# One block for the three programs of each engine, in a kernel of cached cross-attention, self-attention and a mixture of experts

## The chip, the cores and the metric

The kernel runs on one core of one Trainium2 chip. A core has five engines that each run a program of their own: TensorE (PE in the rows, with its weight loads as PEld), VectorE (DVE), ScalarE (ACT), GpSimd (POOL) and SyncE (SP), which here only issues DMAs. They order their work among themselves by semaphores. The metric is the device time of one execution in microseconds (us), taken as the median of several; lower is better.

## The reference, cut to what matters

```python
# 1. cross-attention of 512 rows of x to a context of 8192 rows, width 1024
Q, K_new, V_new = x @ Wq.T + bq, x @ Wk.T + bk, x @ Wv.T + bv      # x is layer-normed first
K = concat(ctx[:7680], K_new); V = concat(ctx[:7680], V_new)       # the last 512 rows are replaced
h = x + softmax(Q @ K.T / sqrt(1024) + mask) @ V
# 2. causal self-attention, 16 query and 4 key heads of 64, low-rank additions, rotary positions
h = h + self_attention(layernorm(h))
# 3. shared feed-forward (relu squared, 2048 wide) + 2 of 16 experts (512 wide) a token
out = h + shared(layernorm(h)) + routed_experts(layernorm(h))
```

All is float32. A product is made of three passes of a rounded kind: each operand is split in a high part, made by ACT with a copy, and a low part, made by DVE as the difference (`_hi`, `_lo`), and the product is high·high + high·low + low·high (L32, L33 and L34 of the helper `matmul_3pass`).

## The kernel before, in words

The kernel is written by hand, engine by engine. Three functions are called in a row: `cross_projections` (V, Q and K of the 512 rows; tiles are named a_...), `attention` (64 steps over 16 context blocks of 512 rows and 4 query blocks of 128 rows, then the self-attention; names b_... and c_...), and `ffn` (names d_... and e_...). Each opens a `with nc.Block() as block:` (L157, L585, L1682) and gives in it one program to each engine (`@block.sync`, `@block.gpsimd`, `@block.tensor`, `@block.scalar`, `@block.vector`). The order of the work in such a program is written out; no scheduler changes it. At the end of a block every engine drains and meets the others at a barrier, and only then does each branch into its program of the next block. I call these two places the first border (around 155 us) and the second border (around 1127 us).

What stands around the first border. The projections run in 12 half-groups; the last two make the K of the 512 rows, feature tiles 4 to 7. For each output tile PE signals `out_ready`, DVE adds the bias (L376) into `a_tmp`, ACT makes the high part (L311), DVE the low part (L379), and the latter counts in the semaphore `out_lo`: 8 V pieces, 8 Q tiles and 8 K tiles make 24. `a_tmp` and the bias rows `a_bv_rows` lie in the same memory as the mask tiles `b_scores`. POOL ends its program by storing four blocks of low-rank-corrected weights (L211). In `attention`, POOL first loads four mask tiles (L626), clears a tile (L627) and goes on with tables; PE begins step 0 of the scores, which goes over the 8 feature tiles f of K and Q (`scores`, L737 onward); SP waits for `kv_split` before it loads more of the cache (L590).

What stands around the second border. PE turns the last 128 rows of the normed hidden state (`turn_xn`, L996); ACT (L1169) and DVE (L1406) split them, and `xt_lo_done` reaches 8. In `ffn`, PE makes the router's logits for these rows (`route_rows`, L423 and L424, 16 products of 128 columns), then the first half of `unit(0)`, which is 12 products, then it turns the logits (`turn_logits`, L1823), and for that it waits until ACT has copied them from PSUM (L2040). ACT's program of `ffn` begins with `shared_hi(2)` (L1986), the high part of the third piece of the shared weights, and the copy of the logits stands behind it. SP's program of `ffn` begins with the load of that piece, `load_shared(2)` (L1688), which waits for the low part of piece 0 (`s_split`, made by DVE at L1411 in `attention`), then piece 3, then the store of the normed rows (L1715). The last DMAs of SP in `attention` are the loads of pieces 0 and 1 (L621).

The lines that the steps touch:

```python
                pe.wait_ge(s["xt_lo_done"], 2 * TB)
                route_rows(pe, bank[:, LOGIT_BANK, :], F, 3 * P, T).then_inc(s["logits_ready"], 1)
...
                shared_hi(2)
                act.wait_ge(s["logits_ready"], 1)
                act.activation(lT, bank[:, LOGIT_BANK, :], ACT.Copy).then_inc(s["lg_read"], 1)
                shared_hi(3)
```

Of the kernel before, what the change touches and what calls it, by code (L numbers as in the profile page):

```python
# [14 lines left out]
P = 128  # L15
# [86 lines left out]
def cross_projections(nc, m, ins, resid, QT, K, V, raw, at, kv_loaded, ident, ln, weff, weff_stored):  # L102
# [23 lines left out]
    with ExitStack() as stage:  # L126
# [30 lines left out]
        with nc.Block() as block:  # L157
            @block.sync
            def _(sp):
                def load_x(t):  # L160
                    sp.dma_start(resid[:, t, :], ins["x"][t]).then_inc(x_loaded[t], 16)

                def load_half(h):
                    sp.dma_start(raw[:, 0, h * D:(h + 1) * D],
                                 ins["xattn_w"][0][:, h * D:(h + 1) * D]).then_inc(w_first if h == 0 else w_loaded[0], 16)

                load_x(0)
                load_x(1)
                load_half(0)
                load_x(2)  # L170
                load_half(1)
                load_x(3)
                for w in range(1, HALVES):
                    if w >= 2:
                        sp.wait_ge(w_split, w + 2)
                    sp.dma_start(raw[:, w % 2, :], ins["xattn_w"][w]).then_inc(w_loaded[w % 2], 16)
                for n in range(2):
                    sp.wait_ge(w_split, HALVES + 2 + n)
                    sp.dma_start(raw[:, n, :], ins["kv"][n]).then_inc(kv_loaded[n], 16)

            @block.gpsimd
            def _(pool):
                pool.memset(consts[:, 0:1], LN_EPS).then_inc(consts_done, 1)
                pool.memset(consts[:, 1:2], -0.5).then_inc(consts_done, 1)
                make_identity(pool, ident, ident_done)
                pool.wait_ge(consts_done, 2)

                def first_weights_lo(j):
                    pool.wait_ge(w_hi_done, j + 1)
                    pool.tensor_tensor(w_buf(K_lo, 0)[:, j, :], w_feature(raw, 0, j), f32(w_buf(K_hi, 0)[:, j, :]),  # L190
                                       ALU.subtract).then_inc(w_split, 1)

                ln.rstd(pool, 0, mean_var, rstd, consts, 0)
                ln.rstd(pool, 0, mean_var, rstd, consts, 1)
                first_weights_lo(0)
                first_weights_lo(1)
                ln.rstd(pool, 0, mean_var, rstd, consts, 2)
                first_weights_lo(2)
                first_weights_lo(3)
                ln.rstd(pool, 0, mean_var, rstd, consts, 3)  # L200
                pool.dma_start(b_cols[:, :], ins["xattn_b_cols"]).then_inc(bias_loaded, 16)
                pool.dma_start(bv_rows[:, :], ins["xattn_bv"].to_broadcast([P, D])).then_inc(bias_loaded, 16)
                pool.dma_start(stack_mask[:, :], ins["stack_mask"][:, 2:4]).then_inc(bias_loaded, 16)
                pool.dma_start(p_raw[0:3 * RANK, :, :], ins["attn_p"]).then_inc(bias_loaded, 16)
                for n in range(4):
                    if n:
                        pool.wait_ge(weff_stored, 16 * n)
                    pool.dma_start(w_block[:, :, :], ins["attn_w"][6 + n].rearrange("p (b n) -> p b n", n=W)
                                   ).then_inc(block_loaded, 16)
                    pool.wait_ge(low_done, LOW_SPLIT + 4 * n + 4)  # L210
                    pool.dma_start(weff[n].rearrange("p (b n) -> p b n", n=W), w_block[:, :, :]).then_inc(weff_stored, 16)  # L211

            @block.tensor
            def _(pe):
                pe.wait_ge(ident_done, 2)

                def turn_x(t):
                    pe.wait_ge(ln.xn_done, t + 1)
                    for h in range(2):
                        n = 2 * t + h  # L220
                        if n >= 2:
                            pe.wait_ge(xt_lo_done, n - 1)
                        for i in range(4):
                            e = 4 * h + i
                            mm = pe.transpose(bank[:, 6 + n % 2, i * P:(i + 1) * P],
                                              resid[:, t, e * P:(e + 1) * P], ident[:, :])
                        mm.then_inc(xt_ready, 1)

                def low_products(n):

                    if n == 0:
                        pe.wait_ge(low_done, LOW_SPLIT)
                    pe.wait_ge(biased, 4 * n + 4)
                    for i in range(4):
                        e = 4 * (n % 2) + i
                        pe.matmul(bank[:, 4 * (n % 2) + i, :], p_s[0:3 * RANK, 0, e * P:(e + 1) * P],
                                  p_s[0:3 * RANK, 1, (n // 2) * W:(n // 2 + 1) * W],
                                  start=True, stop=True).then_inc(low_ready, 1)

                turn_x(0)  # L240
                turn_x(1)
                for w in range(HALVES):
                    g, h = divmod(w, 2)
                    if h == 1 and 1 <= g <= 4:
                        low_products(g - 1)
                    if w:
                        pe.wait_ge(w_split, w + 4)
                    for i in range(4):
                        o = 4 * g + i
                        if h == 0 and g >= 2:  # L250
                            pe.wait_ge(biased, o - 7)
                            pe.wait_ge(low_done, LOW_SPLIT + o - 7)
                        if g == 1 and h == 0 and i >= 2:
                            pe.wait_ge(xt_lo_done, 2 * TB)
                        if g == 0:
                            pe.wait_ge(xt_lo_done, 2 * i + h + 1)
                        for j in range(4):
                            e = 4 * h + j
                            if w == 0:
                                pe.wait_ge(w_split, j + 1)  # L260
                            if g >= 2:
                                lhs = [w_buf(x, w)[:, j, i * P:(i + 1) * P] for x in (K_hi, K_lo)]
                                rhs = [xT_hi[:, e, :], xT_lo[:, e, :]]
                            else:
                                lhs = [x[:, e, i * P:(i + 1) * P] for x in (xT_hi, xT_lo)]
                                rhs = [w_buf(x, w)[:, j, :] for x in (K_hi, K_lo)]
                            mm = matmul_3pass(bank[:, 4 * (g % 2) + i, :], *lhs, *rhs,
                                              first=e == 0, last=e == DB - 1)(pe)
                        if h == 1:
                            mm.then_inc(out_ready, 1)  # L270
                        if w == 0 and i < 2:
                            turn_x(i + 2)
                    if h == 0:
                        mm.then_inc(w_used, 1)

            @block.scalar
            def _(act):
                def weights_hi(w):
                    act.wait_ge(w_loaded[w % 2], 16 * (w // 2 + 1))
                    if w >= 2:  # L280
                        if w % 2 == 0:
                            act.wait_ge(w_used, w // 2)
                        else:
                            act.wait_ge(out_ready, 4 * (w // 2))
                    act.activation(w_buf(K_hi, w), raw[:, w % 2, :].rearrange("p (e n) -> p e n", n=W),
                                   ACT.Copy).then_inc(w_hi_done, 1)

                def first_weights_hi(j):
                    act.wait_ge(w_first if j < 2 else w_loaded[0], 16)
                    act.activation(w_buf(K_hi, 0)[:, j, :], w_feature(raw, 0, j), ACT.Copy).then_inc(w_hi_done, 1)  # L290

                first_weights_hi(0)
                first_weights_hi(1)
                for n in range(2 * TB):
                    t, h = divmod(n, 2)
                    if n == 2:
                        first_weights_hi(2)
                    if n == 3:
                        first_weights_hi(3)
# [2245 lines left out]
```

## Time and profile before

| | us |
|---|---|
| median of 3 runs | 1452.84 |
| the three runs | 1451.96, 1455.63, 1452.84 |
| the profiled execution | 1451.73 |
| its span, from the first to the last instruction | 1450.1 |
| PE busy in it | 1408.3 (97%) |
| DVE, ACT, POOL busy | 845.6, 530.3, 202.8 |

The profiled execution took 1.63 us more than its span, and 1.11 us less than the median of the three runs. PE is busy in nearly all of the span; each instruction of it starts before the one ahead has ended by the profile's model, so a steady run of products of 512 columns shows a start every 0.23 us, while one is listed with 0.39 us. Time on PE's path is therefore counted from start to start.

### The profile page before, as it was taken

The page shows a single profiled execution, that of the slowest core. Times are in us where ns is not written, and L with a number is a line of the kernel's source. Part 1 is how long each engine was busy: PE and PEld are TensorE (multiplying, and loading weights), DVE is VectorE, ACT ScalarE, POOL GpSimd, SP SyncE. Part 2 cuts the span into 40 slices and gives each one's busy share as a digit, 9 for nine tenths or more (in the row PEclk, how much of TensorE's full clock was granted, in tenths as well). Part 3 has the DMA queues.
Part 4 walks back from the last instruction along what each step waited for, and adds up shares of the span by engine and source line. Part 5 has one row for each costly group of instructions (what it writes and reads, how often), then busy time and mean ns, then how long its engine had stood idle before and what let it go on. Part 6 is the DMA issues. An engine that isn't in the chain of part 4 may idle for free. (4 is left out here: it accounts for less than half of the span.)

```text
span 1450.1 us, 18196 instructions
## 1 busy us (share of the span) xinstructions
PE 1408.3 (97%) x6676; PEld 1151.2 (79%) x6676; DVE 845.6 (58%) x1232; ACT 530.3 (37%) x947; POOL 202.8 (14%) x264
## 2 busy tenths in 40 slices
PE   7999999999999999999999999899999899998998
PEld 5878788888888888888888888776778788887786
DVE  5554455555555455455554557678765676676655
ACT  3222322332223322223222223556432435665561
POOL 3000100000000000000000000455311022122132
PEclk9999999999999999999999999999999999999999
DMA  7453643333333333333333322201100566886766
GB/s 251 152 202 118 247 176 118 116 109 108 123 123 111 113 108 115 131 108 116 108 112 131 108 98 77 107 1 59 34 1 1 175 210 228 299 294 222 266 224 218
DMA packets 43487, 203.64 MB, mean 140 GB/s; under 512 B 5233, under 2 KB 5297, under 8 KB 31985
## 3 DMA queue, kind: packets, MB, share of 16 engines
q1 hardware_dynamic: 30016, 152.32, 30.1%
q0 software_dynamic: 9568, 36.35, 7.7%
q10 hardware_dynamic: 3840, 14.16, 2.5%
q8 instruction: 37, 0.61, 0.2%
q14 instruction: 26, 0.20, 0.0%
HBM read 182.36 MB, written 20.45 MB: 140 GB/s over the span
## 5 line engine op out<-in xcount | busy, mean ns | idle before, releaser
L32 PE MATMUL banks<-V_hi,b_PT_hi 128*128 128x512 f32 x512 | 205.6, 401 | 0.0
L1024 ACT ACTIVATE b_PT_hi<-banks 128x512 fp32r<-128x512 f32 x64 | 38.3, 599 | 446.9 <-PE banks L757 446.9
L32 PE MATMUL banks<-K_hi,QT_hi 128*128 128x512 f32 x512 | 199.3, 389 | 2.5 <-PEq L157 2.5
L34 PE MATMUL banks<-V_hi,b_PT_lo 128*128 128x512 f32 x512 | 200.2, 391 | 0.0
L33 PE MATMUL banks<-V_lo,b_PT_hi 128*128 128x512 f32 x512 | 199.6, 390 | 0.0
L34 PE MATMUL banks<-K_hi,QT_lo 128*128 128x512 f32 x512 | 199.4, 389 | 0.0
L33 PE MATMUL banks<-K_lo,QT_hi 128*128 128x512 f32 x512 | 199.2, 389 | 0.0
L1247 DVE TENSOR_TENSOR b_scores<-banks,b_scores 128x512 f32<-128x512 f32 x64 | 44.2, 691 | 202.0 <-PE banks L34 202.0
L642 POOL DMA_DIRECT2D b_scores<-mask x60 | 32.2, 537 | 639.2 <-PE banks L757 621.4
L2176 DVE TENSOR_TENSOR e_lo<-e_raw,e_hi 128x1024 fp32r<-128x1024 f32 x80 | 95.2, 1231 | 38.4 <-ACT e_hi L2012 37.3
L32 PEld LDWEIGHTS banks<-K_hi,QT_hi 128*128 128x128 f32 x512 | 96.1, 188 | 22.8 <-issue 2.9
L34 PEld LDWEIGHTS banks<-V_hi,b_PT_lo 128*128 128x128 f32 x512 | 96.1, 188 | 21.0
L34 PEld LDWEIGHTS banks<-K_hi,QT_lo 128*128 128x128 f32 x512 | 96.1, 188 | 20.0
L33 PEld LDWEIGHTS banks<-K_lo,QT_hi 128*128 128x128 f32 x512 | 96.1, 188 | 19.9
L33 PEld LDWEIGHTS banks<-V_lo,b_PT_hi 128*128 128x128 f32 x512 | 96.4, 188 | 18.5
L32 PEld LDWEIGHTS banks<-V_hi,b_PT_hi 128*128 128x128 f32 x512 | 96.2, 188 | 18.0
L1267 DVE TENSOR_TENSOR V_lo<-raw,V_hi 128x2048 fp32r<-128x2048 f32 x30 | 68.8, 2292 | 64.4 <-ACT V_hi L1048 64.4
L1267 DVE TENSOR_TENSOR K_lo<-raw,K_hi 128x2048 fp32r<-128x2048 f32 x30 | 68.8, 2293 | 61.8 <-ACT K_hi L1048 61.8
L2012 ACT ACTIVATE e_hi<-e_raw 128x1024 fp32r<-128x1024 f32 x80 | 81.4, 1060 | 23.0 <-DMA e_raw<-w_down 16.1
L1204 DVE SCALAR_TENSOR_TENSOR resid<-resid,b_alpha,banks 128x1024 f32<-128x1024 f32 x60 | 76.5, 1275 | 6.8 <-PE banks L34 6.8
L32 PE MATMUL banks<-K_hi,V_hi 128*128 128x512 f32 x160 | 68.2, 427 | 0.8 <-ACT c_piece L1069 0.8
L34 PE MATMUL banks<-K_hi,V_lo 128*128 128x512 f32 x160 | 64.0, 400 | 0.0
(327 smaller groups left out, 2752.4 us busy)
## 6 DMA issues: line engine op xcount, KB each, us to landing
raw<-kv SPq DMA_DIRECT2D x60, 1024.0 KB, 4.7
e_raw<-w_up SPq DMA_DIRECT2D x40, 512.0 KB, 5.0
e_raw<-w_down SPq DMA_DIRECT2D x40, 512.0 KB, 5.9
b_scores<-mask POOLq DMA_DIRECT2D x64, 256.0 KB, 2.9
d_s_raw<-shared_w SPq DMA_DIRECT2D x32, 512.0 KB, 4.9
raw<-xattn_w SPq DMA_DIRECT2D x11, 1024.0 KB, 4.9
y_dram<-c_zeros ACTq DMA_DIRECT2D x1, 6656.0 KB, 28.0
raw<-attn_w SPq DMA_DIRECT2D x6, 1024.0 KB, 4.7
```

The source lines that it names most:

```text
L32: pe.matmul(out, lhs_hi, rhs_hi, start=first, stop=False)
L33: pe.matmul(out, lhs_hi, rhs_lo, start=False, stop=False)
L34: return pe.matmul(out, lhs_lo, rhs_hi, start=False, stop=last)
L642: pool.dma_start(s_sb[:, u, :], ins["mask"][it * 4 + u]).then_inc(mask_loaded[u], 16)
L1024: act.activation(PT_hi[:, u % 2, :], T_ps[:, u % 2, :], ACT.Copy).then_inc(b["pt_hi"], 1)
L1204: op = dve.scalar_tensor_tensor(resid[:, qb, :], resid[:, qb, :], alpha[:, qb:qb + 1], O_ps(u), ALU.mult, ALU.add)
L1247: dve.tensor_tensor(s_sb[:, u % 4, :], S_ps[:, u % 2, :], s_sb[:, u % 4, :], ALU.add).then_inc(b["masked"], 1)
L1267: dve.tensor_tensor(split_tile(False, u), raw_tile(u), f32(split_tile(True, u)), ALU.subtract).then_inc(b["kv_split"], 1)
L2012: act.activation(e_hi[:, first + j, :], e_raw[:, j, :], ACT.Copy).then_inc(s["e_hi"], 1)
L2176: dve.tensor_tensor(e_lo[:, first + j, :], e_raw[:, j, :], f32(e_hi[:, first + j, :]), ALU.subtract).then_inc(s["e_split"], 1)
```

## The change

The three `with nc.Block()` are replaced by one block that is opened in `build` and handed to the three functions. The second and third programs of an engine follow its first without drain and barrier. Where the first barrier had kept apart reads and writes of the same memory, waits on `out_lo` (handed over as `own_split`) are added: PE waits in step 0 before each feature tile, and POOL before each of the four first mask loads. Nothing is added at the second border. The diff, without the change of indentation (all lines of the functions' bodies keep their order):

```diff
-def cross_projections(nc, m, ins, resid, QT, K, V, raw, at, kv_loaded, ident, ln, weff, weff_stored):
+def cross_projections(nc, block, m, ins, resid, QT, K, V, raw, at, kv_loaded, ident, ln, weff, weff_stored):
...
-        with nc.Block() as block:
             @block.sync
...
+        return out_lo
...
-        with nc.Block() as block:
             @block.sync
...
             @block.gpsimd
             def _(pool):
                 for u in range(4):
+                    pool.wait_ge(own_split, 8 if u < 2 else 21 + u)
                     pool.dma_start(s_sb[:, u, :], ins["mask"][u]).then_inc(mask_loaded[u], 16)
...
                     for f in range(DB):
+                        if known == 0:
+                            pe.wait_ge(own_split, 17 + f)
                         mm = matmul_3pass(S_ps[:, u % 2, :],
...
-        with nc.Block() as block:
             @block.sync
...
+            block = stage.enter_context(nc.Block())
+            own_split = cross_projections(nc, block, m, ins, resid, QT, K, V, raw, at, kv_loaded, ident, ln, weff, weff_stored)
             d, F = ffn_semaphores(m), ffn_tiles(m, at, stage)
             F["bank"] = m.psum("banks", [P, 8, W], stack=stage)
-            attention(nc, m, ...)
-            ffn(nc, m, ...)
+            attention(nc, block, m, ..., own_split)
+            ffn(nc, block, m, ...)
```

On PE at the first border, before: the last products of the projections, the two branches with the barrier between them, and the first products of step 0.

```order
L33 MATMUL a_banks<-V_lo,K_hi 128x512
L34 MATMUL a_banks<-V_hi,K_lo 128x512
L157 UNCONDITIONAL_BRANCH
L737 UNCONDITIONAL_BRANCH [waits barrier_Pool_Activation_PE_DVE_SP_release]
L32 MATMUL banks<-K_hi,QT_hi 128x512
L33 MATMUL banks<-K_lo,QT_hi 128x512
L34 MATMUL banks<-K_hi,QT_lo 128x512
L32 MATMUL banks<-K_hi,QT_hi 128x512
```

And the same place of the changed kernel:

```order
L33 MATMUL a_banks<-V_lo,K_hi 128x512
L34 MATMUL a_banks<-V_hi,K_lo 128x512
L737 UNCONDITIONAL_BRANCH
L32 MATMUL banks<-K_hi,QT_hi 128x512 [waits a_out_lo]
L33 MATMUL banks<-K_lo,QT_hi 128x512
L34 MATMUL banks<-K_hi,QT_lo 128x512
L32 MATMUL banks<-K_hi,QT_hi 128x512 [waits a_out_lo]
```

One branch and the barrier are gone; each feature tile of step 0, one in three products, has a wait of its own.

On SP at the second border, before (d_s_raw holds the pieces of the shared weights as loaded):

```order
L621 DMA d_s_raw<-shared_w 128x1024 [waits c_qk_ready]
L621 DMA d_s_raw<-shared_w 128x1024
L585 UNCONDITIONAL_BRANCH
L1683 UNCONDITIONAL_BRANCH [waits barrier_Pool_Activation_PE_DVE_SP_release]
L1688 DMA d_s_raw<-shared_w 128x1024 [waits d_s_split] x2
L1715 DMA xn_dram<-e_raw 128x4x1024 [waits ln_xn_done]
```

And in the changed kernel, where the lines have other numbers:

```order
L620 DMA d_s_raw<-shared_w 128x1024 [waits c_qk_ready]
L620 DMA d_s_raw<-shared_w 128x1024
L1684 UNCONDITIONAL_BRANCH
L1689 DMA d_s_raw<-shared_w 128x1024 [waits d_s_split] x2
L1716 DMA xn_dram<-e_raw 128x4x1024 [waits ln_xn_done]
```

The loads of pieces 2 and 3 now stand behind `s_split` alone, and no longer behind the barrier too.

## Rows read from the trace of the kernel before

**Rows 1.** Span of the core and mean granted clock of TensorE.
```profile
core 0: 1450.1 us, clock 0.994
```

**Rows 2.** Waits of PE: who waited for whom, total us, times, longest.
```profile
PE banks L32 <- DVE d_s_lo L2155: 5.9, 2, 4.7
PE banks L32 <- PEq L157: 2.5, 1, 2.5
...
PE banks L1823 <- ACT e_xg L2040: 1.2, 1, 1.2
```

**Rows 3.** PE in order of time: start, us, operation [idle before <- releaser].
```profile
134.07 0.39 PE L34 MATMUL a_banks<-V_hi,K_lo 128*128 128x512 f32 x1
134.30 0.39 PE L32 MATMUL a_banks<-V_hi,K_hi 128*128 128x512 f32 x1
...
153.11 0.39 PE L34 MATMUL a_banks<-V_hi,K_lo 128*128 128x512 f32 x1
156.00 0.47 PE L32 MATMUL banks<-K_hi,QT_hi 128*128 128x512 f32 x1 [2.50 <-PEq L157]
```

**Rows 4.** Line 157, the first border: ns min/median/max, first and last start.
```profile
L157 PEldq DRAIN  x1: 4267/4267/4267, 149.3 to 149.3; - x1
L157 PEldq EVENT_SEMAPHORE  x1: 51/51/51, 155.9 to 155.9; - x1
```

**Rows 5.** DVE before the first border: low parts of K tiles 6 and 7.
```profile
152.27 0.69 DVE L379 TENSOR_TENSOR K_lo<-a_tmp,K_hi 128x512 fp32r<-128x512 f32 x1 [0.70 <-ACT K_hi L311]
...
154.98 0.69 DVE L379 TENSOR_TENSOR K_lo<-a_tmp,K_hi 128x512 fp32r<-128x512 f32 x1 [0.70 <-ACT K_hi L311]
```

**Rows 6.** POOL at the first border.
```profile
156.40 2.13 POOL L626 DMA_DIRECT2D b_scores<-mask  x4 [33.07 <-POOLq L157]
```

**Rows 7.** PE at the second border, in order of time.
```profile
1125.40 1.09 PE L996 MATMUL banks<-ident,e_raw 128*128 128x128 f32 x8 [0.69 <-DVE e_raw L96]
1128.34 0.30 PE L423 MATMUL banks<-d_xT_hi,e_hi 128*128 128x128 f32 x1 [1.85 <-PEq L585]
...
1130.15 0.45 PE L32 MATMUL banks<-d_xT_hi,d_s_hi 128*128 128x512 f32 x1
...
1132.71 0.39 PE L34 MATMUL banks<-d_xT_hi,d_s_lo 128*128 128x512 f32 x1
1134.29 0.66 PE L1823 MATMUL banks<-ident,e_xg 128*128 128x128 f32 x4 [1.19 <-ACT e_xg L2040]
```

**Rows 8.** DVE at the second border.
```profile
1118.13 2.35 DVE L1411 TENSOR_TENSOR d_s_lo<-d_s_raw,d_s_hi 128x1024 fp32r<-128x1024 f32 x2
...
1126.72 1.29 DVE L1406 TENSOR_TENSOR d_xT_lo<-banks,d_xT_hi 128x512 fp32r<-128x512 f32 x2 [1.38 <-ACT d_xT_hi L1169]
```

**Rows 9.** ACT at the second border.
```profile
1126.09 1.08 ACT L1169 ACTIVATE d_xT_hi<-banks 128x512 fp32r<-128x512 f32 x2 [7.06 <-PE banks L996]
1132.70 1.06 ACT L1986 ACTIVATE d_s_hi<-d_s_raw 128x1024 fp32r<-128x1024 f32 x1 [5.52 <-DMA d_s_raw<-shared_w]
1133.66 0.58 ACT L2040 ACTIVATE e_xg<-banks 128x512 f32<-128x512 f32 x1
```

**Rows 10.** The chain that ended last, in order of time: start, us, what.
```profile
1128.30 4.38 DMA d_s_raw<-shared_w
...
1276.34 0.47 PE banks L32
...
1304.06 0.24 PE banks L34
...
1322.10 0.80 PE banks L32
```

**Rows 11.** Windows: us, busy us of PE, PEld, DVE, ACT, POOL, granted clock, DMA.
```profile
943.00:946.00 3.00, 3.00 (x8) 2.06 (x7) 1.72 (x4) 2.71 (x20) 1.99 (x2) 0.50 0.00 0
...
1322.00:1325.00 3.00, 2.90 (x7) 2.21 (x8) 1.78 (x3) 2.53 (x4) 0.00 (x0) 0.50 0.42 165
153.00:156.00 3.00, 0.50 (x3) 0.10 (x2) 1.44 (x2) 0.63 (x1) 0.00 (x0) 1.00 0.00 0
```

More of the change, by code:

```diff
@@ new lines, in after, with project @@
+            def after(n):
+                transpose(0, n - 1, n - 1)
+                values(0, n - 2, n - 2)
+                turn_x(0)
+                values(0, n - 1, n - 1)
+                turn_x(1)
+            passes(pe, step, after)
+            def project(g, t, first, last, out):
+                rows = slice(t * P, (t + 1) * P)
+                for e in range(first, last):
+                    pe.wait_ge(s["w_split"], 2 * g + e // 4 + 1)
+                    mm = matmul_3pass(out, xT_hi[:, e, rows], xT_lo[:, e, rows],
+                                      K_hi[:, g % 2, e, :], K_lo[:, g % 2, e, :],
+                                      e == 0, g >= 3 and e == DB - 1)(pe)
+                return mm
@@ new lines, in low_rank, with project_low @@
+            def low_rank():
+                pe.wait_ge(s["table_split"], 1)
+                pe.wait_ge(s["xt_lo"], 2 * TB)
+                pe.wait_ge(b["acc_done"], STEPS)
+                for e in range(DB):
+                    mm = matmul_3pass(bank[:, 6, :], A_hi[:, e, :], A_lo[:, e, :], xT_hi[:, e, :], xT_lo[:, e, :],
+                                      e == 0, e == DB - 1)(pe)
+                mm.then_inc(s["lr_ready"], 1)
+            def project_low(i):
+                g, t = ORDER[i]
+                out, rows = piece_bank(i), slice(t * P, (t + 1) * P)
+                if i == 0:
+                    pe.wait_ge(s["lr_lo"], 2)
+                    pe.wait_ge(s["table_split"], 3)
+                mm = pe.matmul(out, lr_s[:, rows], B_s[:, g, :], start=False, stop=g == 0)
+                if g:
+                    mm = pe.matmul(out, lr_lo[:, rows], B_m[:, g, :], start=False, stop=True)
+                mm.then_inc(s["out_ready"], 1)
@@ new lines, in heads_transpose @@
+            def heads_transpose(u):
+                pe.wait_ge(s["s_exp"], u + 1)
+                if u >= 1:
+                    pe.wait_ge(s["pt_act"], u)
+                    pe.wait_ge(s["pt_dve"], u)
+                else:
+                    pe.wait_ge(s["qk_read"], 5)
+                for h in range(2):
+                    for k in range(keys_of(u) // P):
+                        mm = pe.transpose(bank[:, h, k * P:(k + 1) * P],
+                                          p_sb[:, u % 2, h, k * P:(k + 1) * P], ident[:, :])
+                mm.then_inc(s["pt_ready"], 1)
@@ new lines, in heads_values @@
+            def heads_values(u):
+                g = 2 * (u % PAIRS) // GROUP
+                pe.wait_ge(s["pt_act"], u + 1)
+                pe.wait_ge(s["pt_dve"], u + 1)
+                if u == 0:
+                    pe.wait_ge(s["piece_copied"], AHEAD)
+                k = 2 * (u + 2)
+                if not slot_read(pe, k) and not slot_read(pe, k - 1) and u >= 1:
+                    pe.wait_ge(s["y_done"], u)
+                keys = keys_of(u) // P
+                for h in range(2):
+                    for k in range(keys):
+                        mm = pe.matmul(bank[:, Y_BANK, h * HD:(h + 1) * HD],
+                                       pT_sb[:, u % 2, h, k * P:(k + 1) * P], v_sb[:, k, g * HD:(g + 1) * HD],
+                                       start=k == 0, stop=k == keys - 1)
+                mm.then_inc(s["y_ready"], 1)
@@ new lines, in turn_y, with slot @@
+            def turn_y(n):
+                t, h = divmod(n - 2 * TB, 2)
+                pe.wait_ge(s["y_out"], HKV * (t + 1))
+                for i in range(4):
+                    e = 4 * h + i
+                    mm = pe.transpose(xt_bank(n)[:, i * P:(i + 1) * P], y[:, t, e * P:(e + 1) * P], ident[:, :])
+                mm.then_inc(s["xt_ready"], 1)
+            def slot(k):
+                if k not in PIECE_SLOTS.values() and k not in ROWS_SLOTS.values():
+                    return
+                step = k // 2
+                if k % 2 or not slot_read(pe, k - 1):
+                    if step - 1 - (k % 2 == 0) >= 1:
+                        pe.wait_ge(s["y_done"], step - 1 - (k % 2 == 0))
+                for i, at_slot in PIECE_SLOTS.items():
+                    if at_slot == k:
+                        turn_piece(i)
+                for n, at_slot in ROWS_SLOTS.items():
+                    if at_slot == k:
+                        turn_y(n)
@@ new lines, in fill @@
+            def fill(st, part):
+                n, third = divmod(st if st < 3 * FILLED else st - 1, 3)
+                if st == 3 * FILLED:
+                    return
+                blocks_of = FILL_PARTS[third][part]
+                for e in blocks_of:
+                    if n >= FILLED:
+                        output(n - FILLED, e, e + 1)
+                        continue
+                    i = AHEAD + n
+                    g, t = ORDER[i]
+                    if e == 0:
+                        pe.wait_ge(s["piece_copied"], i if n else TB)
+                    mm = project(g, t, e, e + 1, bank[:, FILL_BANK, :])
+                    if e == DB - 1:
+                        if t == TB - 1:
+                            mm.then_inc(s["group_done"], 1)
+                        project_low(i)
@@ new lines, in output @@
+            def output(o, first, last):
+                t, c = divmod(o, 2)
+                for e in range(first, last):
+                    if e % 4 == 0:
+                        pe.wait_ge(s["xt_lo"], 2 * TB + 2 * t + e // 4 + 1)
+                    if e == 0:
+                        pe.wait_ge(s["add_done"], min(o, 2 * TB - 2)) if o else pe.wait_ge(s["piece_copied"], PIECES)
+                    mm = project(3 + c, t, e, e + 1, out_bank(o))
+                if last == DB:
+                    mm.then_inc(s["out_ready"], 1)
```

3374 lines of the change are left out of this document (1633 added, 1741 removed).

## The prediction, made before the changed kernel had run

> **What bounds the kernel now.** I read the granted clock and span first, then PE's waits, then the two borders on every engine in order of time, then the chain that ended last. The span is 1450.1 us at a mean granted clock of 0.994 [rows 1], and PE is busy in 97% of it, so the end is set by PE's own stream and only what moves that stream counts. PE's waits are few. Two of them are the borders, 2.5 us released by the semaphore of line 157 and 1.85 us by that of line 585, and 1.2 us stand at the turning of the logits, behind ACT [rows 2, 7]. The larger wait for the shared weights, 5.9 us in two pieces, lies much later. In the 64 steps of cached attention between the borders the waits of PE name nothing, so what PE gains at the first border has nothing in the loop that would take it back.
>
> **First border: removed.** The last product of the projections starts at 153.11, the first of the scores at 156.00 [rows 3]. In a steady run starts are 0.23 apart (134.07 and 134.30 in the same group), so without the border the next start would be 153.34: 156.00 - 153.34 = 2.66 us on PE's path. What held PE was DVE, whose low part of the last K tile ran 154.98 to 155.67 [rows 5], then its drain and the barrier, released at 155.9 [rows 4].
>
> **First border: added waits.** PE now waits in step 0 before each feature tile. Tile f needs f + 17 counts. Each tile is three products, 0.68 us, so tile 6 is reached at 153.34 + 6 x 0.68 = 157.4, and it needs DVE's tile 6, which ended at 152.27 + 0.69 = 152.96; tile 7 is reached at 158.1 and needs the one that ended at 155.67 [rows 5]. The margin is 2.4 us, so none of the eight is late. What a wait that is already met costs: the product at 134.30 has two such waits, on the bias and on the low-rank sums, and starts 0.23 after the one ahead, like its neighbours [rows 3]. I take zero; behind a waiting tile only PE's own following products are queued. The bounds are 0 and, were the last tile late after all, the 2.66 gained here, since DVE's time sets when PE can go on.
>
> POOL's four mask loads get waits too. Before, they were issued from 156.40 on, 2.13 us for the four [rows 6]. Mask 0 and 1 need 8 counts, reached long before; mask 2 needs 23 (152.96) and mask 3 needs 24 (155.67). So all four go out earlier than before. Behind the fourth are POOL's clearing of a tile and with it ACT's filling of `y_dram`, and the tables; SP waits for a semaphore of the attention steps either way. The clearing follows mask 3, so it comes 156.40 + 2.13 - (155.67 + 0.53) = 2.3 us earlier, where PE comes 2.66 earlier: no engine falls behind by more than 0.4 us, and PE reads nothing of it for a long time. Cost nothing; cover if this fails: the two whole score steps before PE needs the first result of DVE and ACT.
>
> **First border: the branch.** One branch stays on each engine. PE's first product of the scores starts at 156.00, the barrier's event is listed at 155.9 with 51 ns [rows 4], so a branch into the next program has cost PE at most 0.1 us there. PE's sequencer also ran ahead: its drain started at 149.3, while PE's last product started at 153.11 [rows 3, 4]. So some 3.8 us of a late branch would be hidden now. I take zero, with 0 and 0.1 as bounds from these rows. The Trainium skill, "Runtime: NRT & Kernel Launch", section "Instruction fetch mechanics", speaks against the change here: it says that a taken branch whose target is outside the pages held makes the sequencer fetch code before it goes on. By that rule the barrier might have been the cover of such a fetch. The rows show the branch behind the barrier, and no such stall after it.
>
> **Second border: removed.** PE turns eight blocks from 1125.40 and begins the logits at 1128.34 [rows 7]. But their first product also waits for the low parts of these rows, and DVE makes them from 1126.72 to 1128.01 [rows 8]. From ACT's end at 1133.66 + 0.58 to PE's start at 1134.29 there are 0.05 us [rows 7, 9]; with that or a little more the start becomes 1128.1 and the gain is 0.24 us, not the 1.85 that the row of the wait shows. Bounds: 0 (another 0.3 us of signal) and 0.33 (no delay).
>
> **Second border: the logits.** This is the step that isn't seen in the row of the border. PE's twelfth product of unit 0 starts at 1132.71, so the turning of the logits could start at 1132.94; it starts at 1134.29 [rows 7]: 1.35 us lost. PE waits for ACT's copy of the logits at 1133.66, and this stands behind ACT's high part of piece 2 at 1132.70, which waited for its load [rows 9]. SP issued that load at 1128.30, right after the barrier, and it took 4.38 us [rows 10]. In the changed kernel the load waits only until DVE is done with piece 0, the first of two that ran from 1118.13 for 2.35 us [rows 8], so it is issued at about 1119.4 and lands at about 1123.8 (all in the old times). ACT ends its last split of rows at 1126.09 + 1.08 = 1127.17 [rows 9], makes the high part of piece 2 until 1128.2, and copies the logits as soon as PE has made them. These are 16 products from 1128.1 on. Unit 0 starts at 1132.71 + 0.23 - 12 x 0.23 = 1130.2 before, so at about 1129.9 now; the copy takes 0.58 and is done by 1130.7, two microseconds before PE asks for it at 1132.7. The gain is the whole 1.35. Bounds: 0, if the copy is late all the same, and 1.35.
>
> More is earlier behind it: the low parts of pieces 2 and 3, the routing on DVE and the loads that follow come some 3 to 5 us earlier against PE's 4. The first of PE's two waits on line 2155 ends at 1276.34, far behind [rows 10], so that brings nothing, and the store of the normed rows beside them delays nothing of PE either.
>
> **Is it given back?** The largest wait of PE behind this, 4.7 us up to 1322.10, is fed by a load; the chain goes from PE's product at 1304.06 through ACT, DVE, SP and a DMA back to PE [rows 10]. Such a chain begins at PE, so it moves with PE and the gain stays. I give nothing back.
>
> **Sum.** 2.66 + 0.24 + 1.35 = 4.25 us. The profiled execution took 1451.73 (its span and 1.63 around it), so it would take 1447.5; the median of the runs shown, 1452.84, lies 1.11 above it and would become 1448.6. I predict 1448.0, halfway, since I cannot say which of the two executions the next ones resemble.
>
> **The rivals.**
> - The clock gives more. In 943 to 946 and in 1322 to 1325 PE ran at a granted clock of 0.50, the lower of the two levels (1.2 GHz), the second right after the wait of 4.7 us; between 153 and 156, with PE busy 0.50 of 3 us, the clock stayed at 1.00 [rows 11]. The mean of 0.994 makes (1 - 0.994) x 2 x 1450 = 17 us at the lower clock, 9 us lost. The runs shown differ by 3.7 us, and I take that for such stretches. In an execution where the pause of a border did lower the clock, the change removes that too: 3.4 us at half speed, 1.7 us lost, is my estimate from these windows, each of which is half speed over its whole 3 us. Then 1447.5 - 1.7 = 1445.8, and down to 1445.0 with two. The Trainium skill, "TensorE: Matmul & The Clock Gate", part 1, says that the chip's looking is not aligned with the kernel, so one and the same pause may or may not lower the clock; this case's one trace can neither show nor refute it.
> - Only part of it. If ACT still reaches the logits late (a load delayed, the copy behind something else), only 2.66 + 0.24 is gained: 1448.8 to 1449.9. The row of ACT's load wait, 5.52 us long [rows 9], speaks for the full gain; the margin of two microseconds would have to go.
> - The change doesn't do what it says: PE stops at tile 7, because DVE's last low part comes later than before, or the gain is swallowed at 1322. Then 1451.7 to 1452.8. DVE has nothing new to do at the border and the chain starts at PE, both against it.
> - Slower: the clock goes the other way. All of PE's later pauses shift by 2.7 to 4.3 us against whatever lowers the clock, and where a pause now keeps the clock up it may lower it. The place is the self-attention from 880 to 1110 and the expert chunks, where PE pauses often. It costs 1.7 us a stretch, and decides against the change from the third additional one on: 1448.0 + 3 x 1.7 = 1453.1. Nothing in the rows says that a shift favours more stretches over fewer.
>
> **How the numbers follow.** Full gain with the clock as before: 0.62, own range 1446.6 to 1449.6. More from the clock: 0.16. Part of it: 0.14. No gain: 0.04. Slower through the clock: 0.04. A measurement of this kernel can tell about 0.3% from no change, 4.4 us, which puts the line at 1448.5, right beside my forecast. Of the full gain I put two thirds below it, 0.41; with the 0.16 that makes 0.57 for faster. The rest of the full gain, the partial and the missing gain, and most of the slower case, which only passes +0.3% (1457.2) with five or more stretches, make 0.41 for the same; 0.02 for slower. The range for 8 in 10: 1445.3 to 1450.6, which leaves out the missing gain, the slower case and the end of the clock's.
>
> **What would show it.** On PE, products 0.23 us apart from the projections into the scores, no wait on line 157's semaphore, and no wait on `out_lo`; SP's load of piece 2 about 9 us before the turning of the last rows is done; PE's wait at the logits gone, and a start of them about 0.1 us after DVE's last low part; the wait before the shared weights in the fifth chunk still there, some 4.3 us earlier in the span. I am wrong if PE stops in step 0, if ACT's copy of the logits is still what PE waits for, or if PE's waits later than 1250 grow by what was gained.

## The result, and the profile after

| | before | changed |
|---|---|---|
| median of 9 executions, us | 1452.20 | 1447.86 |
| lowest and highest | 1450.29, 1455.63 | 1446.55, 1452.75 |
| profiled execution | 1451.73 | 1449.44 |
| its span and mean granted clock | 1450.1, 0.994 | 1447.5, 0.991 |

The ratio is 0.997, with a 95% interval from 0.9958 to 0.9983: 4.3 us faster, where 4.25 were summed and 1448.0 was predicted. The whole interval lies below 1, so the gain is real, though it is right at the 0.3% that I had set as the bound.

The span of the profiled execution fell by only 2.6 us, and its clock is lower. So the size can't be read off the two spans; it has to be taken apart by steps. The lines of the changed kernel have other numbers than before (L422 and L423 are the logits, L1824 their turning, L626 the mask loads, L378 the low part of the K tiles).

The first border, PE in order of time, answers to [rows 3]:

```profile
152.77 0.39 PE L33 MATMUL a_banks<-V_lo,K_hi 128*128 128x512 f32 x1
153.00 0.39 PE L34 MATMUL a_banks<-V_hi,K_lo 128*128 128x512 f32 x1
153.23 0.39 PE L32 MATMUL banks<-K_hi,QT_hi 128*128 128x512 f32 x1
153.45 0.39 PE L33 MATMUL banks<-K_lo,QT_hi 128*128 128x512 f32 x1
...
157.99 0.39 PE L32 MATMUL banks<-K_hi,QT_hi 128*128 128x512 f32 x1
158.21 0.39 PE L33 MATMUL banks<-K_lo,QT_hi 128*128 128x512 f32 x1
```

The scores follow 0.23 us behind the projections, and feature tile 7, reached at 157.99, starts without a pause. DVE's low part of that tile, which answers to [rows 5], and POOL's last two mask loads, which answer to [rows 6], in order of time:

```profile
154.88 0.69 DVE L378 TENSOR_TENSOR K_lo<-a_tmp,K_hi 128x512 fp32r<-128x512 f32 x1 [0.70 <-ACT K_hi L310]
```

```profile
153.15 0.54 POOL L626 DMA_DIRECT2D b_scores<-mask  x1 [28.86 <-DVE K_lo L378]
155.87 0.54 POOL L626 DMA_DIRECT2D b_scores<-mask  x1 [2.18 <-DVE K_lo L378]
156.40 0.97 POOL L627 MEMSET c_zeros<- 128x1024 f32 x1
```

DVE is done at 155.57, 2.4 us before PE needs the tile.

The second border, PE in order of time, answers to [rows 7]:

```profile
1120.84 1.09 PE L998 MATMUL banks<-ident,e_raw 128*128 128x128 f32 x8 [0.70 <-DVE e_raw L96]
1123.51 0.33 PE L422 MATMUL banks<-d_xT_hi,e_hi 128*128 128x128 f32 x1 [1.57 <-DVE d_xT_lo L1408]
...
1126.15 0.63 PE L34 MATMUL banks<-d_xT_hi,d_s_lo 128*128 128x512 f32 x1
1126.58 0.63 PE L32 MATMUL banks<-d_xT_hi,d_s_hi 128*128 128x512 f32 x1
...
1129.74 0.60 PE L1824 MATMUL banks<-ident,e_xg 128*128 128x128 f32 x4
```

From the turned rows to the first logit there are 2.67 us, before 2.94: 0.27 gained, and the pause of 1.57 us that is left is DVE's, no longer the barrier's. The wait at the turning of the logits is gone. But the products ahead of it are 0.43 us apart instead of 0.23, so from the first logit to the turning there are 6.23 us, where before there were 5.95 with the wait in them. ACT, which answers to [rows 9], and SP at the same place:

```profile
1121.53 1.09 ACT L1171 ACTIVATE d_xT_hi<-banks 128x512 fp32r<-128x512 f32 x2 [7.06 <-PE banks L998]
1122.51 1.06 ACT L1987 ACTIVATE d_s_hi<-d_s_raw 128x1024 fp32r<-128x1024 f32 x1
1125.55 0.60 ACT L2041 ACTIVATE e_xg<-banks 128x512 f32<-128x512 f32 x1 [1.98 <-PE banks L423]
```

```profile
1114.81 1.46 SPq L1689 DMA_DIRECT2D d_s_raw<-shared_w  x2
```

ACT no longer waits for the load of piece 2, since SP issues it at 1114.81, and its copy of the logits waits for PE alone. Windows of the changed kernel, which answer to [rows 11] (us, busy us of PE, PEld, DVE, ACT and POOL, granted clock, DMA share, GB/s):

```profile
153.00:156.00 3.00, 3.00 (x15) 2.49 (x14) 1.44 (x2) 0.63 (x1) 0.67 (x2) 1.00 0.27 87
1126.00:1128.00 2.00, 2.00 (x6) 1.51 (x6) 0.88 (x1) 1.09 (x2) 0.00 (x0) 0.50 0.97 299
1153.00:1156.00 3.00, 3.00 (x9) 2.35 (x8) 2.40 (x10) 1.06 (x1) 0.00 (x0) 0.50 0.13 46
1317.00:1323.00 6.00, 5.09 (x12) 3.89 (x13) 4.76 (x5) 5.53 (x6) 0.00 (x0) 0.50 0.32 99
```

The lower of the two levels (1.2 GHz) stands in the stretch right behind the pause of the second border, in another some 27 us later, and for 6 us at 1317 instead of 3 at 1322. Neither of the first two was in the profile before. In the other direction, a stretch of 3.4 us at 991 that the profile before had is missing here. Against the profile before that makes some 6 us more at the lower clock, up to 3 us lost, and this is where the execution lost what its span lacks.

PE's waits (who for whom, total, times, longest) answer to [rows 2]:

```profile
PE banks L32 <- DVE d_s_lo L2156: 4.7, 2, 4.4
...
PE banks L422 <- DVE d_xT_lo L1408: 1.6, 1, 1.6
```

Neither border's semaphore is named any more. The wait for the shared weights is still there.

### The profile page after: what moved, and what is told of

It reads as the page before. It is cut to its first block and busy times, and to the rows that moved or that the text cites. A ratio compares the mean times of both kernels' runs of the same rounds, so it can differ in the third digit from the quotient of the medians.

```text
span 1447.5 us, 18174 instructions
## 1 busy us (share of the span) xinstructions
PE 1411.2 (97%) x6676; PEld 1154.1 (80%) x6676; DVE 846.9 (59%) x1232; ACT 530.2 (37%) x947; POOL 203.1 (14%) x264
```

## The experiments

### The first border alone, and the second alone

```diff
+            with nc.Block() as block:
                 own_split = cross_projections(nc, block, ...)
...
                 attention(nc, block, ..., own_split)
+            with nc.Block() as block:
                 ffn(nc, block, ...)
```

> Projections and attention in one block, the feed-forward in a block of its own: only the first border is gone. My theory: the products of the scores follow 0.23 us after the last of the projections (saving 2.66 us), the second border stays with PE's start 0.3 us behind DVE's last low part, and PE waits 1.2 us at the turning of the logits as before; median 2.7 us under the kernel before. Rival (the borders cost only together, or the barrier moves its wait elsewhere): less than 1 us.

Measured: 1449.45 us (8 executions), ratio to the kernel before on the same chip 0.9977, interval 0.9960 to 0.9995, so 3.3 us faster, with 2.7 inside the interval. The first border behaved as expected (152.82, then 153.04). PE at the second:

```profile
1119.09 1.09 PE L998 MATMUL banks<-ident,e_raw 128*128 128x128 f32 x8 [0.70 <-DVE e_raw L96]
1122.04 0.30 PE L422 MATMUL banks<-d_xT_hi,e_hi 128*128 128x128 f32 x1 [1.85 <-PEq L2472]
1128.24 0.60 PE L1824 MATMUL banks<-ident,e_xg 128*128 128x128 f32 x4
```

The barrier's pause of 1.85 us is there as before. One thing I had expected is not: PE doesn't wait at the turning of the logits, although this border is kept and ACT's copy is as late as ever (it starts 5.4 us behind the first logit, before 5.3). There are 6.20 us between the two lower rows, as many as in the changed kernel within 0.03.

```diff
             with nc.Block() as block:
                 cross_projections(nc, block, ...)
...
             with nc.Block() as block:
                 attention(nc, block, ...)
                 ffn(nc, block, ...)
```

(without the added waits)

> The projections in a block of their own, attention and feed-forward in one: only the second border is gone, and none of the added waits is there. My theory: PE waits 2.5 us at the first border as before; at the second PE starts the logits 0.1 us after DVE's last low part instead of 0.33 us, and the wait of 1.2 us at their turning is gone, 1.6 us in all. Rival (the second border is worth the 1.85 us that its row shows, and the logits' wait is ACT's own): the start comes 1.85 us earlier against the end of the turned rows, and 1.2 us of wait stay.

Measured: 1453.93 us (10 executions), ratio 1.0005, interval 0.9991 to 1.0018. The 1.6 us are not seen; the interval ends at 1.3 us of gain. PE in this kernel:

```profile
1125.85 0.33 PE L422 MATMUL banks<-d_xT_hi,e_hi 128*128 128x128 f32 x1 [1.57 <-DVE d_xT_lo L1405]
...
1128.53 0.63 PE L33 MATMUL banks<-d_xT_lo,d_s_hi 128*128 128x512 f32 x1
1128.95 0.63 PE L34 MATMUL banks<-d_xT_hi,d_s_lo 128*128 128x512 f32 x1
...
1132.10 0.60 PE L1821 MATMUL banks<-ident,e_xg 128*128 128x128 f32 x4
```

All steps of the border are as predicted (a pause of 1.57 us, no wait at the turning), but again the products are 0.42 us apart, and 6.25 us lie between logit and turning. So in these two profiled executions the stretch costs the same, with the border or without it. The two rivals in the expectations don't explain that; the clock does, below.

### The load's place, and ACT's order, with both borders kept

```diff
                 for i in range(2):
                     sp.dma_start(F["s_raw"][:, i, :], ins["shared_w"][i]).then_inc(d[f"s_loaded{i}"], 16)
+                for i in range(2):
+                    sp.wait_ge(d["s_split"], i + 1)
+                    sp.dma_start(F["s_raw"][:, i, :], ins["shared_w"][2 + i]).then_inc(d[f"s_loaded{i}"], 16)
...
-                load_shared(2)
-                load_shared(3)
```

> The kernel before with both borders kept, but SP issues the loads of pieces 2 and 3 of the shared weights at the end of its attention program, behind the low parts of pieces 0 and 1. My theory: the start of the logits stays 0.3 us behind DVE's last low part (border kept), PE's wait of 1.2 us at their turning is gone: 1.35 us gained from the load's place alone. Rival (the barrier itself makes ACT late): the wait stays at about 1.2 us.

```diff
-                shared_hi(2)
                 act.wait_ge(s["logits_ready"], 1)
                 act.activation(lT, bank[:, LOGIT_BANK, :], ACT.Copy).then_inc(s["lg_read"], 1)
+                shared_hi(2)
```

> The kernel before with both borders, but ACT copies the logits before it makes the high part of piece 2. My theory: the copy was late only because it stood behind an instruction that waited for a load, so PE's wait of 1.2 us at the turning is gone though the load is as late as before (issued at the barrier, 4.4 us). Rival (the load itself, or the copy, is what takes the time): the wait stays.

One execution of each, 1456.04 and 1451.74 us. In neither does PE wait at the turning (1128.48 to 1134.70 and 1126.56 to 1132.75, 6.22 and 6.19 us). That is what both expectations say of the wait, but it proves little, since the first-border kernel has no wait there either while its copy is late. These two settle that each edit makes the copy early. The 1.35 us that were expected of the load's place are not shown: one time of each kernel, and in the first a mean clock of 0.989, the lowest of all profiled executions. ACT in the kernel with the early load, where the copy waits for PE alone:

```profile
1128.46 1.06 ACT L1987 ACTIVATE d_s_hi<-d_s_raw 128x1024 fp32r<-128x1024 f32 x1 [1.15 <-PEq L585]
1131.18 0.60 ACT L2041 ACTIVATE e_xg<-banks 128x512 f32<-128x512 f32 x1 [1.66 <-PE banks L424]
```

They show something at the first border, which they keep. The kernel with the copy first, in two windows:

```profile
152.00:155.00 3.00, 1.58 (x7) 0.96 (x6) 1.44 (x2) 0.91 (x2) 0.00 (x0) 1.00 0.00 0
156.00:159.00 3.00, 2.91 (x7) 2.37 (x8) 0.00 (x0) 0.00 (x0) 2.51 (x5) 0.50 0.39 113
```

The pause of the border is followed by the lower clock here. In the profile before it was not, with the same pause [rows 3, 11]:

```profile
156.00:159.00 3.00, 3.00 (x13) 2.52 (x14) 0.00 (x0) 0.00 (x0) 2.60 (x5) 1.00 0.44 153
```

### What the pause at the first border was

```diff
-                        pe.wait_ge(own_split, 17 + f)
+                        pe.wait_ge(own_split, 24)
```

> The changed kernel, but PE waits before the first feature tile of step 0 for all 24 low parts instead of one tile at a time. My theory: the pause at the first border was DVE's tail, 2.3 us, and only 0.3 us the drain and barrier; so PE starts the scores about 0.05 us after DVE's last low part, some 2.4 us later than in the changed kernel, and nearly the whole gain of this border is gone. Rival (the drain and the barrier are the price): PE starts at once or within 1 us.

One execution, 1452.55 us. PE and DVE at the border:

```profile
153.33 0.39 PE L34 MATMUL a_banks<-V_hi,K_lo 128*128 128x512 f32 x1
155.95 0.50 PE L32 MATMUL banks<-K_hi,QT_hi 128*128 128x512 f32 x1 [2.23 <-DVE K_lo L378]
```

```profile
155.21 0.69 DVE L378 TENSOR_TENSOR K_lo<-a_tmp,K_hi 128x512 fp32r<-128x512 f32 x1 [0.70 <-ACT K_hi L310]
```

PE starts at 155.95, 0.05 us behind DVE's end and 155.95 - 153.56 = 2.39 us later than it could. Set against the 2.66 us before, the barrier and its drains were 0.27; 2.39 were the tail of ACT and DVE, and it is the wait tile by tile that gives them back. One block with a single coarse wait would have gained next to nothing at this border. The one time doesn't size this; the rows do.

### The clock behind the second border

```diff
+            shared_split(pe, 0)
+            for e in range(6):
+                pe.matmul(bank[:, 0, :], s_hi[:, 0, e * P:(e + 1) * P], s_hi[:, 0, 0:W], start=True, stop=True)
             pe.wait_ge(s["xt_lo_done"], 2 * TB)
```

> The changed kernel with six products of 512 columns, written to a bank that unit 0 overwrites, in PE's pause before the last logits. They leave the output as it is. They take 6 x 0.23 = 1.4 us of a pause of 1.57 us, so they delay PE by 0 to 0.1 us. Theory: the lowered clock of 3.4 us that follows this pause in the changed kernel's profile comes from the pause; with it filled, no stretch of lowered clock begins between the turned rows and unit 0, and the median is 0 to 1.7 us lower. Rival (it comes from the light stretch around it, or from elsewhere): the lowered stretch is there in this run too, and the median is the same.

Measured: 1444.64 us (12 executions), ratio 0.9953, interval 0.9934 to 0.9973; 3.2 us under the changed kernel, 2.8 under its repetition on another chip. PE:

```profile
1121.56 1.63 PE L1907 MATMUL banks<-d_s_hi 128*128 128x512 f32 x6
1123.38 0.33 PE L422 MATMUL banks<-d_xT_hi,e_hi 128*128 128x128 f32 x1 [0.18 <-DVE d_xT_lo L1408]
...
1127.33 0.39 PE L32 MATMUL banks<-d_xT_hi,d_s_hi 128*128 128x512 f32 x1
1127.56 0.39 PE L33 MATMUL banks<-d_xT_lo,d_s_hi 128*128 128x512 f32 x1
...
1128.02 0.60 PE L1824 MATMUL banks<-ident,e_xg 128*128 128x128 f32 x4
```

The pause is 0.18 us, the clock stays up, and there are 4.64 us from logit to turning. The median moved by more than the 0 to 1.7 us expected: the stretch some 27 us later, at 1153 in the changed kernel, is gone here as well, and two such stretches are 2 x 1.6 = 3.2 us. The size is less sure than the medians look. The twelve times run from 1442.91 to 1455.33, they come from another chip than the repetition of the changed kernel, and the ratio's interval overlaps that of the changed kernel (0.9958 to 0.9983). That the clock is higher with the filler is seen in the means: 0.9943 over these twelve, 0.9924 over the 21 of the changed kernel.

```profile
1126.00:1128.00 2.00, 2.00 (x10) 1.61 (x9) 1.01 (x1) 0.96 (x2) 0.00 (x0) 1.00 0.98 281
1148.00:1152.00 4.00, 4.00 (x31) 3.77 (x31) 1.91 (x8) 2.55 (x4) 0.00 (x0) 1.00 0.64 223
```

To tell the clock from the wait, the same filler went into the kernel with only the first border gone, ahead of the barrier that it keeps.

```diff
                 turn_xn(3)
+                pe.wait_ge(d["s_split"], 1)
+                for e in range(6):
+                    pe.matmul(bank[:, 0, :], F["s_hi"][:, 0, e * P:(e + 1) * P], F["s_hi"][:, 0, 0:W], start=True, stop=True)
```

> Only the first border gone (the feed-forward in a block of its own), with the same six filling products at the end of PE's attention program, ahead of the barrier; they leave the output as it is. It separates the clock from the logits' wait. My theory: with the first border alone gone, PE's wait at the turning of the logits was hidden by the lowered clock, which made PE 1.7 us late itself; with the pause filled the clock stays up, and the wait of 1.2 us behind ACT is back. From the first product of the last logits to the turning: 5.9 us, against 4.6 us in the changed kernel with the filler. Rival (the wait depends on something else): no wait, 4.6 us.

Measured: 1449.31 us (10 executions), ratio 0.9971, interval 0.9959 to 0.9983. PE, and ACT:

```profile
1121.78 0.30 PE L422 MATMUL banks<-d_xT_hi,e_hi 128*128 128x128 f32 x1 [0.46 <-PEq L2475]
1128.39 0.66 PE L1827 MATMUL banks<-ident,e_xg 128*128 128x128 f32 x4 [1.82 <-ACT e_xg L2044]
```

```profile
1126.79 1.06 ACT L1990 ACTIVATE d_s_hi<-d_s_raw 128x1024 fp32r<-128x1024 f32 x1 [6.19 <-DMA d_s_raw<-shared_w]
1127.76 0.58 ACT L2044 ACTIVATE e_xg<-banks 128x512 f32<-128x512 f32 x1
```

With the clock up the wait is back: 1.82 us (the load took 0.6 us longer than before), 6.61 us from logit to turning against 4.64 with the second border gone and the same filler. So the step is real, 1.3 to 2.0 us, but only where the clock stays up. Where it falls, PE itself is 1.6 us late, and ACT's lateness is hidden under it. The times fit that: the mean clock rose from 0.9916 with the first border alone to 0.9937 with the filler added, and yet the median stayed (1449.45 and 1449.31 us), since the wait took back what the clock gave.

> The changed kernel once more, on the chip of these runs, as the measure for the other two: 1447 to 1449 us. By my theory a lowered stretch of 3.4 us follows the pause at the second border, so PE takes 6.2 us from the first of the last logits to their turning; where it doesn't come, 4.6 us.

Measured: 1447.44 us (12 executions), ratio 0.9970, interval 0.9957 to 0.9984, the first result again. In its profiled execution the clock stayed up at this place:

```profile
1122.11 0.33 PE L422 MATMUL banks<-d_xT_hi,e_hi 128*128 128x128 f32 x1 [1.57 <-DVE d_xT_lo L1408]
1126.74 0.60 PE L1824 MATMUL banks<-ident,e_xg 128*128 128x128 f32 x4
```

4.63 us, the other of the two values expected. The same program with the same pause of 1.57 us ran once at the lower clock behind it and once not.

### The largest wait of PE, and a faster kernel

```diff
-                load_chunk_down(c + 1, 16 + 8 * c)
                 if c == 4:
                     load_shared(22)
                     load_shared(23)
+                load_chunk_down(c + 1, 16 + 8 * c)
```

> The changed kernel, with the loads of pieces 22 and 23 of the shared weights ahead of the four w_down loads of the same chunk. PE's largest wait before the experts' end, 4.4 us on the low part of piece 22 or 23, is fed by these two loads, which SP holds back behind four loads that wait for DVE. If so, they go out some 7 us earlier, the wait is gone, and with it the 3.4 to 6.8 us of lowered clock right behind it: 4.4 + 1.7 us or more gained, about 1442 us. Rival (another engine is late there too, or the w_down loads become late and PE waits for them instead): under 2 us.

Measured: 1442.48 us (6 executions), ratio 0.9918, interval 0.9895 to 0.9941. SP in the changed kernel, then in this one:

```profile
1304.43 3.73 SPq L1698 DMA_DIRECT2D e_raw<-w_down  x4
1308.22 1.27 SPq L1689 DMA_DIRECT2D d_s_raw<-shared_w  x2
```

```profile
1292.80 10.97 SPq L1689 DMA_DIRECT2D d_s_raw<-shared_w  x4
1306.06 3.73 SPq L1698 DMA_DIRECT2D e_raw<-w_down  x4
```

The two loads are out by 1303.8, before the four that had held them back, and these go out 1.6 us later than in the changed kernel without a wait of PE for them. The clock in the place of the old wait, in this kernel:

```profile
1310.00:1316.00 6.00, 6.00 (x28) 4.99 (x27) 2.96 (x3) 3.25 (x4) 0.13 (x1) 1.00 0.90 330
```

PE is busy through it at the full clock; the wait of 4.4 us and the slow 6 us behind it are both gone. The median is 5.4 us under the changed kernel's, 5.0 under its repetition. The profiled execution also waits 2.15 us for the low part of another shared piece at 1272, where the changed kernel's waited 0.32; this lies ahead of the moved loads, and with the filler below it is 0.52.

> The changed kernel with the loads of pieces 22 and 23 ahead of the w_down loads, and with the six filling products before the last logits, which leave the output as it is. If the two gains are independent: 5.4 us and 3.2 us under the changed kernel's 1447.86, about 1439.3 us. Rival (the clock falls elsewhere instead): about 1442, as with the loads alone.

Measured: 1440.05 us (6 executions, 1436.53 to 1445.11), ratio 0.9913, interval 0.9890 to 0.9937. It is the fastest kernel of the study, 7.4 us under the changed kernel's repetition in the same series. Whether the two gains add up is not shown: by the medians the filler adds 2.4 us to the moved loads, by the ratios, each to the kernel before on its own chip, 0.7, and the intervals overlap almost wholly.

## Why the prediction was right, point by point

**First border, 2.66 us.** Right, with its reasons. Gap, branch and added waits came out as worked out: 0.23 us from the last projection to the first score, no pause at tile 7, a margin of 2.4 us. The bound of 0 to 0.1 us for the branch holds, the row at 153.23 has no room for a stall. The Trainium skill, "Runtime: NRT & Kernel Launch", section "Instruction fetch mechanics", says that a taken branch to code outside the pages held has to wait until it is fetched. This trace shows no such stall at the border; whether the code there lay outside the pages, it doesn't show. With the first border alone gone the times agree: 3.3 us, interval 0.7 to 5.8.

**Second border, 0.24 us.** Right on PE's rows: 0.27. The times of the kernel with this border alone gone can't show so little. The row of the wait, 1.85 us, would have misled; DVE's last low part set the time. One sign was written wrongly: the load of piece 2 was to come "about 9 us before the turning of the last rows is done". The prediction's own numbers give 1126.5 - 1119.4 = 7.1, and 7.1 were measured; 9 is how much earlier it comes than before.

**The logits, 1.35 us.** The mechanism was right: early load, early copy, no wait. As a term of the sum it was sized for the wrong execution. I took it from a profile in which the clock had stayed up behind the second border. Without the filler, the clock fell there in 7 of the 9 profiled executions of this study, the profile before and the repeated one being the two in which it didn't. In the 7 the stretch takes 6.19 to 6.26 us, whether the copy is early or late. So in the more frequent case this term is near nothing. The ten executions with the second border alone gone, which showed no gain, fit that, but their interval would also hold 1.3 us.

**What stood in for it.** The rival "the clock gives more" had 0.16. Every execution of the series has a span and a mean granted clock. Their product is an estimate of what the span would be with no stretch at the lower clock; it counts such time as half lost, where the starts of the products say 0.47. Means of all executions, without one of 4928 us on one chip's kernel before:

| kernel | executions | time, us | clock | span x clock, us |
|---|---|---|---|---|
| before, on three chips | 56 | 1453.2 | 0.9912 | 1438.7 |
| changed, both series | 21 | 1448.5 | 0.9924 | 1435.7 |
| only the first border gone | 8 | 1449.7 | 0.9916 | 1435.9 |
| only the second border gone | 10 | 1453.2 | 0.9909 | 1438.3 |

From before to changed the last column falls by 3.1 us (95% interval 2.3 to 3.8), which is what the two borders were summed at, 2.66 + 0.24 = 2.90. The rest of the fall of the span, 1.8 us (0.8 to 2.8), is time at the lower clock that no longer occurs. So in the mean it is the clock, and not the logits' 1.35, that fills the sum up. A part of it can be placed. At the first border the pause was kept in five profiled executions (before, second border alone, early loads, copy first, coarse wait), and in three of them the lower clock followed, as in the window from 156 to 159 above. Without the pause it never did, in seven. At 1.6 us a time that is about 1.0 us on average over such few. Where the other 0.8 would come from stays open, and so does how much of it is chance. The sum was right partly by luck: a term that counts only sometimes was taken whole, and one that comes only sometimes was left out of the sum.

**A term that was taken as fixed.** The prediction carried the 1.63 us outside the span over unchanged. With both borders they are 1.65 on average (56 executions), with one of them gone 1.70 (18), with both gone 1.87 (21): joining the blocks gives 0.2 us back outside the span. Which part of the start or the end they belong to isn't shown.

**No giving back.** Right in the mechanism. The wait at the shared weights moved with PE: 4.4 us against 4.7. In the ten profiled executions that have it, 6.8 us of lower clock follow in eight and 3.4 in two, one of them the profile before. That this is not the change's doing is seen in the two kernels with both borders kept and the load or the copy moved, which have 6.8 too. PE's last waits, for DVE's additions to the residual rows, are 2.6 us against 2.0, and the first wait for a shared piece is 0.3 against 1.2.

**Rivals.** "Only part of it" was nearer to the truth than its 0.14 says, for the second border, and for a reason that I had put into another rival: not a late copy but a slow PE. "Slower through the clock" didn't come. "No gain" is refuted by the interval.

## What to carry to other kernels

The barrier between two programs of an engine cost mostly the tail of the slowest engine, not itself: 2.39 of 2.66 us here. So joining the programs pays only with waits as fine as the data. Look also for a load that the next program issues first: it is held back by the barrier, and the wait for it stands in another row than the border's. On a kernel that PE bounds, look for what a pause does to the clock behind it before sizing anything around it; a wait of another engine can vanish under a slow PE and come back when PE is fast. And the largest wait on the list that a load feeds is worth a look before the border: one moved pair of loads, on top of the change, brought 5.0 to 5.4 us by the medians, where the change had brought 4.3.

## What the runs showed of the hardware that I had not expected

- The same pause in the same program is followed by the lower clock in one execution and not in another: 6.23 and 4.63 us for the same 28 products in the changed kernel. The Trainium skill, "TensorE: Matmul & The Clock Gate", part 1, says that the looking of the chip isn't aligned with the kernel. These two executions agree with it.
- Six products whose result nobody reads were put into the pause of 1.6 or 1.9 us at the second border. The clock stayed up behind it in all three profiled executions with them, and in two of nine without. The changed kernel's median was some 3 us lower with them; with the second border kept it was the same, since a hidden wait came back.
- The lower stretch behind this pause is followed by a second one, 27 us later, in all seven executions that have it; the two in which the clock stayed up without the filler have neither. Why stays open: in the kernel with only the first border gone and the filler, the first stretch was missing and the second was there:

```profile
1150.80:1154.20 3.40, 3.40 (x11) 2.83 (x11) 2.49 (x10) 1.18 (x2) 0.00 (x0) 0.50 0.59 165
```

- The pause at the first border is 2.2 to 2.5 us and lies between steady products, and the lower clock followed it in three executions of five.
- A product started during the lower clock is 0.43 us from the next, against 0.23 at the full one, less than double. Over a stretch of 3.4 us that loses 1.6 us.
